# Written-out first and last rounds, four chunks of the first expert tile in the last rounds, one logarithm for two divisors

## What is computed

```python
h = tok(x, h0)                                  # two strided convolutions along time
h = h + attn(layernorm(h), Wk, Wr, Wo, time_decay, time_first)
h = h + ffn(layernorm(h), router_w, router_b, W1, b1, W2, b2)

# attn: k = x Wk^T, r = v = x Wr^T, w = -exp(time_decay); per channel over time:
    y  = (e1 * a + e2 * v) / (e1 * b + e2)      # e1, e2: exponentials of pp - q, u + k - q
    out = sigmoid(r) * y  ->  out Wo^T
# ffn: logits = x router_w + router_b; the two best experts, softmax of their scores as gates;
    y_e = relu(x W1_e + b1_e) W2_e + b2_e       # 256 -> 1024 -> 256, fp32
    out = sum over the two experts of gate * y_e
```

## Time and profile before

| | |
|---|---|
| time, median of 3 runs | 968.99 us (968.45 to 974.1) |
| the profiled execution | 974.89 us |
| its span (first to last instruction) | 973.1 us |
| mean granted TensorE clock | 0.971 |
| PE busy | 918.5 us (94%) |
| DVE busy | 776.2 us (80%) |
| ACT busy | 613.6 us (63%) |
| POOL busy | 547.5 us (56%) |

### The profile page before, as it was taken

The page is one execution under the profiler, slowest core; times in us unless marked ns, Lnnn a source line. Parts: engine busy times, 40 slices in busy tenths (PEclk is TensorE's granted clock), DMA queues, the critical chain, the costliest instruction groups (busy, mean ns, idle before and its releaser), DMA issues. The chain is left out here.

```text
span 973.1 us, 17357 instructions
## 1 busy us (share of the span) xinstructions
PE 918.5 (94%) x5838; PEld 785.2 (81%) x5838; DVE 776.2 (80%) x2020; ACT 613.6 (63%) x1182; POOL 547.5 (56%) x463
## 2 busy tenths in 40 slices
PE   5999999999964999999999999999999999999996
PEld 3567676667644899999989989999999999999895
DVE  3799999999895877777867878797787777879774
ACT  2899999999872455555645645565565564556452
POOL 1003565667574556556756655775665676567553
PEclk9999999999775899999999999999999999999998
DMA  9664454562141345545556554556554665655643
GB/s 263 236 212 164 136 167 133 157 234 81 50 140 66 126 127 146 140 126 138 144 178 179 148 143 126 163 145 208 139 149 139 189 175 138 138 147 145 208 51 36
DMA packets 73297, 144.33 MB, mean 148 GB/s; under 512 B 9069, under 2 KB 62430, under 8 KB 69242
## 3 DMA queue, kind: packets, MB, share of 16 engines
q0 software_dynamic: 31136, 99.92, 38.0%
q1 hardware_dynamic: 42074, 43.30, 13.8%
HBM read 111.36 MB, written 31.83 MB: 147 GB/s over the span
## 5 line engine op out<-in xcount | busy, mean ns | idle before, releaser
L1462 ACT ACTIVATE hid<-hp,b 128x512 f32<-128x512 f32 (+1 forms) x248 | 158.3, 638 | 247.8 <-PE hp L1499 247.1
L1511 PE MATMUL acc<-whi,hhi 128*128 128x256 f32 x876 | 246.1, 281 | 0.0
L1511 PE MATMUL acc<-wlo,hhi 128*128 128x256 f32 x876 | 245.9, 281 | 0.0
L1511 PE MATMUL acc<-whi,hlo 128*128 128x256 f32 x876 | 245.6, 280 | 0.0
L1416 POOL DMA_INDIRECT out_rows<-yout,dest x108 | 183.6, 1700 | 42.2 <-issue 32.9
L1499 PE MATMUL hp<-xhi,whi 128*128 128x512 f32 (+1 forms) x496 | 186.4, 376 | 7.2 <-PEq L215 4.3
L1788 DVE CAST hhi<-hid 128x512 fp32r<-128x512 f32 (+1 forms) x240 | 103.0, 429 | 106.2 <-ACT hid L1462 106.2
L1499 PE MATMUL hp<-xlo,whi 128*128 128x512 f32 (+1 forms) x496 | 184.0, 371 | 0.0
L1499 PE MATMUL hp<-xhi,wlo 128*128 128x512 f32 (+1 forms) x496 | 183.4, 370 | 0.0
L1511 PEld LDWEIGHTS acc<-wlo,hhi 128*128 128x128 f32 x876 | 165.4, 189 | 8.3
L1511 PEld LDWEIGHTS acc<-whi,hhi 128*128 128x128 f32 x876 | 164.7, 188 | 8.0
(11 more groups left out here) (219 smaller groups left out, 1481.6 us busy)
## 6 DMA issues: line engine op xcount, KB each, us to landing
frames<-in_x SPq DMA_DIRECT2D x32, 512.0 KB
frames<-in_x SPq DMA_DIRECT2D x32, 256.0 KB
token_rows<-xs SPq DMA_DIRECT2D x16, 388.5 KB, 4.7
out_rows<-h SPq DMA_DIRECT2D x16, 384.0 KB, 2.5
expert_lists<-setup SPq DMA_DIRECT2D x12, 280.0 KB
h<-token_rows,tile_tid POOLq DMA_INDIRECT x110, 5.6
out_rows<-yout,dest POOLq DMA_INDIRECT x110, 4.0
expert_lists<-tokens,slots POOLq DMA_INDIRECT x96, 2.9
```

The lines of the kernel that those rows point to most:

```text
L1462: act.activation(hid[:, c % 2, 0:j.r * P], hp[c % 2][:, 0:j.r * P], ACT.Relu, bias=b1[:, j.s, c:c + 1]).then_inc(hid_done, 1)
L1511: last = pe.matmul(acc_of(j, r), h_[:, c % 4, r * P:(r + 1) * P], w_[j.s][:, at:at + C], start=c == 0 and n == 0 and (r % 2 == 0 or j.last ...
```

## The change

1. **Rounds.** `rounds` now runs `body` for rounds 3 to 14 only. Rounds before and after are written out, per engine, in `first_rounds` and `last_rounds`, call by call with the pair's number. In `body` the calls stand in another order, and some belong to another round: PE's calls are one round later relative to the others (`conv(p1)`, `kr(p3, 2)`), ACT's and DVE's steps of the choice start half a round earlier (`lg_in(p3)`), ACT's `kr(p2, 2)`, `kr(p2, 3)` come at the head of the next round.
2. **One logarithm.** ACT's `sigmoid_divisor` adds 1 by an Identity with a bias tile; DVE's `whole_divisor` multiplies both divisors; ACT takes one logarithm of the product and one exponential with a bias tile. DVE's `sigmoid_divisor` and `log_sum` and ACT's `log_sigmoid` are gone.
3. **Chunks of T0 in the first block.** `first_up` 0 to 3, `first_relu`, `first_high`, `first_low` 0 to 3 and `first_down` 0 and 1 stand in `last_rounds`. The second block starts T0 at chunk 4 (`EARLY`). Banks of PSUM and the tiles hid, hhi, hlo, b1 are shared by both blocks. Of T1's eight weight pieces five (`EARLY_PIECES`) are split during T0, three in T1 itself.
4. **Fetches.** POOL issues T1's weights before the last scatters; in the second block it fetches T2 first and scatters the last pair afterwards; T3's weights come behind its rows. SP stores rows one round earlier.

The core of the diff:

```diff
+EARLY, EARLY_PIECES = 4, 5
-            def log_sigmoid(q):
-                act.wait_ge(state, q.at(N_STATE, STATE['sigmoid_divisor']))
-                act.activation(lner[:, :, :], er[:, :, :], ACT.Ln).then_inc(inv_ready, 1)
+            def sigmoid_divisor(q):
+                act.wait_ge(er_ready, q.at(2, 1))
+                act.activation(er[:, :, :], er[:, :, :], ACT.Identity, bias=c_unit[:, 0:1]).then_inc(er_ready, 1)
 
             def log_divisor(q):
-                act.wait_ge(state, q.at(N_STATE, STATE['divisor']))
-                act.activation(lnd[:, :, :], den[:, :, :], ACT.Ln).then_inc(inv_ready, 1)
+                act.wait_ge(state, q.at(N_STATE, STATE['whole_divisor']))
+                act.activation(den[:, :, :], den[:, :, :], ACT.Ln, scale=1.0 / SCALE).then_inc(inv_ready, 1)
 
             def inverse(q):
-                act.activation(inv[:, :, :], lsum[:, :, :], ACT.Exp, scale=-1.0).then_inc(inv_ready, 1)
+                act.activation(inv[:, :, :], den[:, :, :], ACT.Exp, bias=c_scale[:, 0:1], scale=-1.0).then_inc(inv_ready, 1)
...
-            def sigmoid_divisor(q):
-                dve.tensor_scalar(flat(er[:, :, :]), flat(er[:, :, :]), EMAX, 1.0, ALU.min, ALU.add).then_inc(state, 1)
-            def log_sum(q):
-                dve.tensor_tensor(flat(lsum[:, :, :]), flat(lnd[:, :, :]), flat(lner[:, :, :]), ALU.add).then_inc(state, 1)
+            def whole_divisor(q):
+                dve.wait_ge(er_ready, q.at(2, 2))
+                dve.wait_ge(state, q.at(N_STATE, STATE['divisor']))
+                dve.scalar_tensor_tensor(out=den[:, :, :], in0=er[:, :, :], scalar=EMAX, in1=den[:, :, :],
+                                         op0=ALU.min, op1=ALU.mult).then_inc(state, 1)
...
+            def first_up(c):
+                if c == 0:
+                    pe.wait_ge(kr_taken, 4 * PAIRS)
+                    pe.wait_ge(xlo_done, HC)
+                if c >= 2:
+                    pe.wait_ge(hid_done, c - 1)
+                pe.wait_ge(wlo_done, 2 + 2 * (c * P // PIECE))
...
+                        last = pe.matmul(kr_ps[c % 2][:, 0:TS], w_[:, at:at + P], x_[:, k, :], start=n == 0, stop=n == 3 * HC - 1)
...
             def first():
-                fetch.scatter(Pair(PAIRS - 1), range(6))
                 gather_b2(T0)
...
+                if j.first():
+                    fetch.scatter(Pair(PAIRS - 1), range(6))
...
-                for c in range(FC):
+                for c in range(EARLY if j.first() else 0, FC):
```

More of the change, by code:

```diff
@@ L189, in indices, with rounds @@
     dve.tensor_copy(tables.idx[:, j.i, :].unsqueeze(1), tables.table[:, bass.ds(j.col, 1), :]).then_inc(tables.idx_ready, 1)
-def rounds(body):
+def rounds(body, start, end):
     def pairs(i):
         return [Pair(i - lag) if 0 <= i - lag < PAIRS else None for lag in range(STEPS)]
-    for i in range(PAIRS + STEPS - 1):
+    for i in range(start, end):
         body(*pairs(i))
@@ L591, in body @@
                 if p2:
[L592 to L598 removed]
+                    sigmoid_exp(p2)
+                if p3:
+                    root_2(p3)
                 if p1:
@@ L639, in _ @@
+            first_rounds()
+            rounds(body, 3, PAIRS - 1)
+            last_rounds()
         @block.tensor
@@ L769, in body, with first_rounds @@
-                if p1:
-                    if p1.q == 0:
-                        pe.wait_ge(loaded, 16 * 5)
-                    kr(p1, 0)
-                    kr(p1, 1)
-                    kr(p1, 2)
-                if p0 and p0.last:
-                    first_rows(0)
-            rounds(body)
+            def first_rounds():
+                conv(pair[0])
+                conv(pair[1])
+                transpose_1(pair[0])
+                pe.wait_ge(loaded, 16 * 5)
+                kr(pair[0], 0)
+                kr(pair[0], 1)
@@ L1197, in body @@
-                if p4:
-                    new_ends(p4)
+                if p2:
+                    weighted_sum(p2)
+                if p4 and p4.q == KNOWN - 1:
+                    running_number()
+                if p3:
+                    lg_in(p3)
+                if p2:
+                    numerator(p2)
+                if p3:
+                    best(p3)
+                if p4 and p4.q == KNOWN - 1:
+                    not_reached()
+                if p2:
+                    output(p2)
@@ new lines, in first_rounds @@
+            def first_rounds():
+                for t in range(3):
+                    statistic_1(pair[0], t)
+                for t in range(3):
+                    mean_1(pair[0], t)
+                shift_1(pair[0])
+                for t in range(3):
+                    statistic_1(pair[1], t)
+                for t in range(3):
+                    mean_1(pair[1], t)
+                shift_1(pair[1])
+                running_max(pair[0])
+                difference(pair[0])
+                for t in range(3):
+                    statistic_1(pair[2], t)
+                for t in range(3):
+                    mean_1(pair[2], t)
+                value_now(pair[0])
+                weighted(pair[0])
+                weights_sum(pair[0])
+                shift_1(pair[2])
+                divisor(pair[0])
+                running_max(pair[1])
+                whole_divisor(pair[0])
+                difference(pair[1])
+                weighted_sum(pair[0])
+                numerator(pair[0])
+                output(pair[0])
@@ L1474, in body, with first_tile, relu @@
                         x_high(n, c - x_at)
-            tiles(act, body)
+            def first_tile():
+                def relu(c):
+                    act.wait_ge(hp_done, c + 1)
+                    act.wait_ge(hlo_done, c - 1)
+                    act.activation(hid[:, c % 2, :], hp[c % 2][:, :], ACT.Relu, bias=b1[:, 0, c:c + 1]).then_inc(hid_done, 1)
+                act.wait_ge(w_in[T1.s], 16)
+                w_high(T1, 0)
+                relu(4)
+                w_high(T1, 1)
+                relu(5)
+                w_high(T1, 2)
+                x_high(T1, 0)
+                relu(6)
+                w_high(T1, 3)
+                x_high(T1, 1)
+                relu(7)
+                w_high(T1, 4)
+            first_tile()
+            tiles(act, body, 1)
             gated(LAST)
@@ L1522, in body @@
                         down(j.prev(), c + FC - 2)
-                    if c == (1 if j.small() else 3) and j.nxt().exists():
+                    if c == (1 if j.small() else EARLY if j.first() else 3) and j.nxt().exists():
                         transposes(j.nxt())
```

765 lines of the change are left out of this document (546 added, 219 removed).

## The result

The change makes the kernel slower: 1013.29 us (median of 4 runs, 1012.38 to 1019.55) against 971.51 us (4 runs, 968.45 to 974.1), a ratio of 1.045 with an interval of 1.0415 to 1.0484. (Each ratio is taken over all runs but a few slow ones of the same kernel, so it can differ by some tenths of a percent from that of the two medians, here 1.043.) The profiled execution took 1012.38 us, its span 1010.6. I had forecast 954.5 us, with 963 as the end of the range.

What follows compares the result with a forecast made beforehand. Token rounds were taken as bound by VectorE with ScalarE close behind, expert tiles by TensorE, between them a chain of waits. Terms summed to -16.1 us, 952.9 from the median 968.99; 1.6 given back made 954.5 us, range 944 to 963.

Steps and rivals of the forecast that it cites:

- b: First rounds: ScalarE's copies of pair 0 ahead of the long clamps start pair 1's maximum earlier; -1.5 us.
- a: Steady token rounds: one logarithm shortens each of twelve rounds from 16.17 to about 15.9 us, ScalarE the new bound; -3.5 us.
- a': Three rounds with fetches: GpSimd's gathers and scatters make its key late for the running maximum; +2 us.
- c1: Step from pair 14 to 15: TensorE's wait and low clock go, making it a normal 16.1 us; -3.9 us.
- c2: Drain from pair 15's maximum to the first block's end: early chunks fill idle time, 44 us; -1.8 us.
- d: First expert tile: 8.5 us of chunks leave it, a 1.5 us wait appears at tile 1's head; 16.0 us, -7.4.
- tile loop: Expert tiles from tile 1 to the end: nothing should differ, 633 us.
- The ring: Rival in the token rounds: divisor, logarithm, exponential and output wait on each other, 2.5 us a round, near 988 us; chance 0.04.

Runs made afterwards that it cites:

- e5: The kernel before, unchanged, on a second chip; 969.23 us, ratio 1.0001.
- e7: The changed kernel with SyncE's order of the kernel before (loads two pairs ahead, rows stored at step 5), second chip; 962.98 us, ratio 0.9935.
- e6: The changed kernel, unchanged, on the second chip; 1014.0 us, ratio 1.0466 to the kernel before.
- e9: e7 with GpSimd's gathers of the first tiles' rows behind its key, half a round later; 966.09 us against 974.4 on a third chip, ratio 0.990.
- e4: The kernel before with only SyncE's order of the changed kernel; 984.66 us, ratio 1.0058.
- e11: e9 with VectorE taking tile 1's second row block ahead of the last hidden chunk; 967.47 us against 974.4, ratio 0.987.
- e10: e7 with the early chunks of the first tile put back into the tile itself; 982.95 us, ratio 1.0055.
- e8: The kernel before with only the one logarithm of the product of both divisors, everything else in the old order; 973.47 us, ratio 1.0043.
- e12: The same kernel as e11, run once more; 965.5 us against 974.35, ratio 0.992.
- e1: The same edit as e7 (the changed kernel with SyncE's order of before), on the first chip; 979.89 us, ratio 1.0006.
- e3: The changed kernel with only the loads, and the clearing of the expert lists, one round earlier in SyncE's order; 980.16 us, ratio 1.0021.

## Why the prediction was wrong, step by step

The sum beside what e5 and e7 measured, both on one chip (starts of the maxima 41.30 and 235.02 in e5, 40.66 and 233.60 in e7):

| step | forecast | e7 - e5 |
|---|---|---|
| b, start (maximum of pair 1) | -1.5 | -0.6 |
| a, twelve rounds | -3.5 | -2.7 |
| a', fetch rounds | +2 | +1.9 |
| c1, step from pair 14 to 15 | -3.9 | +0.4 |
| c2, drain | -1.8 | +1.5 |
| d, first tile | -7.4 | -9.0 |
| tile loop | 0 | +1.2 |
| SyncE's queue (e6 - e7, medians) | not in the sum | +51 |

(The maxima of pairs 1 and 9 are 127.99 us apart in e5 and 126.41 in e7, those of pairs 9 and 13 65.73 and 66.53. Step a is the first difference and four times the 0.27 to 0.28 of a steady round; a' is what is left. The round from pair 13 to 14, -0.2, is in none of them; with it the rows up to the tile loop add up to -7.5, the difference of the two spans, 960.9 and 968.4.)

**The step that failed** is one that the prediction doesn't have: it put the change of SyncE's order at nothing, without a reason, and the runs show 51 us for it (e6 against e7). It went through VectorE, ScalarE, TensorE and GpSimd and never through SyncE's order, though the fourth point of the change says that SyncE stores rows a round earlier, and the diff has the loads a round later. A sum over it would have needed three numbers: when the store's last wait ends (with `second_gate`, at the end of VectorE's round), what stands behind the store (the load), and the time from issue to use, 8.6 us in the profile above. The first two follow from the orders and the time line of before; for the third, the first two convolutions there start 9.7 us after the first issue of their loads and wait for them (2.69 to 12.35, 9.02 to 18.74). The ring that I had among the rivals, over the logarithm at 988 us, is on the right side but is another mechanism: e7 has the same logarithm in the same order and a round of 15.89.

**a.** The steady round is 15.89 us (forecast 15.9), from 16.17. The first of the twelve loses 0.3 instead (15.34 against 15.00), hence -2.7. ScalarE's exponential with the bias tile takes 948 ns (844 without), the Identity 929 where the logarithm took 827: 0.10 each, where I had 0.09. By the Trainium skill (ScalarE: Activation LUTs, section What ACT_TABLE_LOAD costs; the prediction names the section that follows it) a pointer operand adds about 93 ns. The runs agree, with 104 and 102 ns. But ScalarE is not the bound alone: VectorE is full too (80.00 of 80 us in e7), ScalarE at 79.69.

**a'.** Size and reason are right: VectorE waits 1.28 us for GpSimd's key in the round with the first lists, and the key costs another 0.57 in the two rounds with the gathers (e9), 1.9 in all. What the prediction had otherwise is where: not up to 1.2 us in each of three rounds by the gathers, but most of it once, by `first_lists`.

**b.** The maximum of pair 1 comes 13.66 us after that of pair 0 in e7 and 12.99 in e5; the new order of the start gains nothing there (13.2 to 13.7 in the ten profiles with the new order; 13.0 to 13.3 in e5, e4 and the first profile of before). The 0.6 us come from an earlier first maximum (27.00 against 28.31), which varies from 26.6 to 30.1 between the profiles.

**c1.** The 20.07 us are not in every execution of the kernel. The kernel before has this step at 16.64 us in e5, and again at 20.07 in e4, whose other engines have the old order; in both TensorE waits 2.17 us for the selection first, and what differs is how long it then has 1.2 GHz (an estimated 3.4 us in e5, from the mean clock of 0.90 over the step; 10.3 us in the earlier trace rows). The new order shows 17.07 us at 0.90 in e7, and 15.5 at 1.00 in the changed kernel and in e11. So the forecast of 16.1 for the new order was near; what was wrong is the value of before. I had noticed that the profile lay 5.9 us above the median and gave 1.6 us back; against e5 the right amount was the whole of c1. Some executions of the kernel before do seem to have the long stall: of the 29 beside e5, 25 took 965.6 to 972.1 us at mean clocks of 0.972 to 0.977 and four 974.2 to 978.1 at 0.966 to 0.969, and of the four beside the result two took 974. That it is this stall in them is not shown; these executions have no trace.

**c2.** The mix of both clock levels that I chose gave 44 us against 45.8; e7 has 46.2, e5 44.7. The clock did rise (0.78 in the drain of e7, 0.64 in e5), but the stretch did not get shorter. I take it that the path runs over VectorE's and ScalarE's steps; e10 and the profiles of before (see there) do not settle how much of the 1.5 us is the order's. Step and drain together are safer to compare, since in the new order a step of 15.5 us comes with a drain of 48.5: 61.3 us in e5, 62.0 in e8, 66.1 and 66.2 in the two profiles of the old order with the long stall, and 62.3 to 64.0 in ten profiles of the new order. The forecast for both was 60.1.

**d.** The step that carries the gain: 14.3 us, 16.0 forecast. The wait at the head of tile 1 is there (2.07 us, 1.5 forecast); what I had too high is the start, which runs at the full clock (1.00 in e7's last row, 0.88 in e5's), so 2.8 us of half clock are gone and not 0.4. The tile loop is the same within 1.2 us, as forecast.

So the mechanism that gains, the chunks, was right; with the queue set right (e7) the kernel comes out at 0.9935 of before, 8.5 us short of my forecast of 954.5, mostly because c1 and c2, forecast at -5.7 us in all with 1.6 given back, came to +1.9 against e5. That d gave 1.6 us more than forecast hides a part of it, and is not to the credit of the sum. Of the kernels run, e9 (0.990), e11 (0.987) and e12 (0.992) have the lowest ratios, and their intervals overlap.

## What to carry to other kernels

When a change moves calls between rounds, write for every queue, the ones that only issue transfers included, which instruction now stands behind which wait, and add issue and transfer time to the next use; a store that waits for the end of a round must not stand ahead of the load that the next round begins with. Before a stall seen in one profile is put into a sum as gain, compare that execution with the median: if it lies above it by about the stall, the stall may be in some executions only. When an experiment gives back only a part of a loss, look at what still stands ahead of the wait before another cause gets the rest.

## What the runs showed of the hardware

- A load of 1.5 MB in four transfers by SyncE's queue, issued over 2.3 us, was used 8.6 us after its first issue in the changed kernel's round at 121 us; one transfer landed 5.7 to 6.3 us after its own issue, while the token rows and the previous output were being stored beside it.
- A wait can cost twice: the convolution of 28 matmuls behind the wait of 3.01 us took 4.93 us at a mean granted clock of 0.65, where in e7 the same 28 take 3.24 us. It does not each time: behind waits of 2.62 us (changed kernel, 190.09) and 2.63 (e6, 109.08) it took 3.24 us at 1.00.
- The same step of the same kernel, behind the same wait of 2.17 us, took 16.64 us (e5) and 20.07 (kernel before as profiled, and e4), with TensorE at 1.2 GHz for an estimated 3.4 us and for 10.3 us.
- The tile loop took 632.3 to 633.8 us in four kernels on one chip (e5 to e8), 636.3 to 645.0 on another (e1 to e4), and 637.1 to 642.1 on a third (e9 to e12); in e1 and e3 there are repeated waits of TensorE of 1.2 to 1.3 us some 83 us apart. What they are due to is not shown.
